# Graph network layer on one core: counting apart from the sort's prefixes, and a strided digit comparison

## What is computed

```python
edge_index = jnp.stack([src, dst])
h = jnp.maximum(_layernorm(x), 0.0)
# attention layer: row = src, col = dst
h = (h @ W).reshape(N, H, C)
alpha = leaky_relu(s_src[row] + s_dst[col])
ex = exp(alpha - m[row])            # m: max(segment maximum by row, 0)
deg = segment_sum(ones(E), row)
denom = segment_sum(ex, row) + (E - deg)[:, None] * exp(-m)
out = segment_sum((ex / denom[row])[:, :, None] * h[col], col) + bias
x = x + out
# second layer: an MLP on (x[row], x[col], edge_attr), summed by row
```

## Time and profile before

| | |
|---|---|
| median of three runs | 5412.68 us |
| profiled execution, its own time | 5404.83 us |
| its span, first to last instruction | 5403.0 us |
| stage 1, start to the first instruction behind its barrier | 297.1 us |
| scatters of stage 2, first start to last start | 316.28 to 2329.63 us |
| mean granted TensorE clock | 0.906 of full |

### The profile page before, as it was taken

How to read it: one execution, slowest core, us unless ns; L and a number is a source line. 1 busy time by engine, 2 the same in 40 slices (tenths; PEclk the granted TensorE clock), 3 DMA queues, 4 the chain that set the end, 5 groups by cost and what they waited for, 6 DMA issues and landing times. The chain is left out here.

```text
span 5403.0 us, 98958 instructions
## 1 busy us (share of the span) xinstructions
PE 4070.9 (75%) x22798; PEld 3396.3 (63%) x22799; DVE 3569.6 (66%) x8071; ACT 3043.6 (56%) x4591; POOL 3250.7 (60%) x3487
## 2 busy tenths in 40 slices
PE   5778777777777777700799987777777777777778
PEld 5766666666666666600799965666666666666666
DVE  8945444444444444429999986777777777777776
ACT  5545555555555555401677756666666666666665
POOL 2357777777777777750000005777777777777774
PEclk9988888888888888855899999999999999999999
DMA  8865555555555554597200046656666666666655
GB/s 311 321 204 151 139 139 140 140 139 141 139 140 142 139 139 139 156 89 19 58 0 0 0 114 162 147 144 147 144 148 144 147 144 147 144 147 144 147 144 134
DMA packets 1212202, 734.52 MB, mean 136 GB/s; under 512 B 929642, under 2 KB 1031204, under 8 KB 1205388
## 3 DMA queue, kind: packets, MB, share of 16 engines
q1 hardware_dynamic: 862700, 336.19, 31.5%
q0 software_dynamic: 131424, 275.52, 17.5%
q10 hardware_dynamic: 218048, 122.49, 7.6%
HBM read 562.32 MB, written 165.09 MB: 135 GB/s over the span
## 5 line engine op out<-in xcount | busy, mean ns | idle before, releaser
L1086 POOL DMA_INDIRECT g_q<-q_d,g_aux x1660 | 1571.3, 947 | 1380.3 <-DMA pw<-g_q 874.7
L577 POOL DMA_INDIRECT rec_d<-rec,place x1568 | 1536.3, 980 | 502.8 <-issue 476.1
L1393 PE MATMUL g_hp<-pw,g_mix 128*128 x3328 | 878.1, 386 | 317.0 <-ACT g_mix L1290 310.8
L690 PE MATMUL lk<-tab_sd,low 128*128 128x196 f32 x3136 | 1050.8, 422 | 0.0
L1404 PE MATMUL g_ap<-g_hid,g_oh 128*128 128x256 f32 x3328 | 876.4, 386 | 133.9 <-DVE agg L1196 129.7
L626 DVE TENSOR_REDUCE rank<-equal 128x4 f32<-128x512 bf16 x392 | 262.4, 684 | 1015.4 <-ACT equal L554 1014.8
L1310 ACT ACTIVATE g_hid<-g_q 128x512 f32<-128x512 f32 x832 | 524.0, 630 | 712.5 <-DVE g_q L1182 699.2
L1393 PEld LDWEIGHTS g_hp<-pw,g_mix 128*128 128x128 f32 x3328 | 617.2, 190 | 475.2 <-issue 399.3
L1182 DVE TENSOR_TENSOR g_q<-g_hp,g_q 128x512 f32<-128x512 f32 x832 | 573.2, 689 | 484.9 <-DMA g_q<-q_d,g_aux 333.9
L687 PE MATMUL lk<-mask,hx 122*128 122x245 bf16 x1568 | 480.0, 306 | 440.2 <-ACT low L543 440.2
L554 ACT ACTIVATE equal<-rk,minus_two 128x512 bf16<-128x512 f32 x392 | 261.5, 685 | 958.9 <-DMA rec_d<-rec,place 643.1
(11 more groups left out here) (251 smaller groups left out, 5035.2 us busy)
## 6 DMA issues: line engine op xcount, KB each, us to landing
low_row<-rows_d SPq DMA_DIRECT2D x392, 256.0 KB
rec_d<-pad ACTq DMA_DIRECT2D x49, 1152.0 KB, 4.3
g_ea<-rec_d SPq DMA_DIRECT2D x208, 256.0 KB, 4.2
rec<-in_ea ACTq DMA_DIRECT2D x196, 256.0 KB
hx_row<-rows_d SPq DMA_DIRECT2D x392, 98.0 KB
g_lrow<-low_row_d SPq DMA_DIRECT2D x208, 128.0 KB, 4.2
g_q<-q_d,g_aux POOLq DMA_INDIRECT x1660, 3.0
rec_d<-rec,place POOLq DMA_INDIRECT x1568
```

The costliest lines, as they stand in the source:

```text
L577: pool.indirect_dma_start(rec_d, bass.IndirectOffsetOnAxis(ap=place[0:n, at, j:j + 1], axis=0), rec[0:n, at, j, :], None).then_inc(s_sc[at ...
L690: mm = pe.matmul(to[:, NB:LK], low[:, par, 1, slots], tab_sd[:, :, :].rearrange("p h a -> p (h a)"), start=False, stop=True, skip_group_ch ...
L1086: pool.indirect_dma_start(qg[:, par, j, :], None, q_d, bass.IndirectOffsetOnAxis(ap=aux[:, par, j, F_IDX - F_LOW:REC - F_LOW].bitcast(I32) ...
L1393: mm = pe.matmul(hp[u][:, k * HID:(k + 1) * HID], mix[:, par, 2 * u + k, :], pw[:, bass.ds(b[k], 1), :].rearrange("p o f -> p (o f)"), sta ...
```

## The change

In stage 1 TensorE now only counts: all 32 matmuls of a step add into one region of 49 PSUM columns (cnt), over all 49 steps, without ever being moved out. The one-hots of 4 groups are made by one pair of VectorE instructions, in two buffers, and the first two steps' pairs stand right behind the source digits, ahead of the statistics. The moves, the stores to pre_d and GpSimd's additions are gone. The prefixes are made in stage 2, one group ahead, from one-hots (ohl, ohh) that VectorE compares with digits held in PSUM; the table addition reads them from PSUM. Groups 0 and 1 are loaded in stage 1, ahead of the h stores. A fill has 26 columns in place of 32, so that SyncE issues 15 of them at the start and ScalarE 49 of the smaller size. The comparison for hx walks its 1024 elements with the 8 columns innermost, a step of 128 elements. Two copies of the record swap places.

```diff
-FILL = 32
+FILL = 26
@@ load_group @@
-                sp.dma_start(pre_in[:, par, :], pre_d[one, :, :].rearrange("o p n -> (o p) n")).then_inc(s_ld[par], 16)
@@ stage 1, sync @@
                     def store(it):
-                        for k in range(FOUR):
-                            g = it * FOUR + k
-                            sp.wait_ge(s_pre, g + 1)
-                            sp.dma_start(pre_d[bass.ds(g, 1), :, :].rearrange("o p n -> (o p) n"), pre[:, k, :]).then_inc(s_ps[k], 16)
                         sp.wait_ge(s_ev, it + 1)
...
+                    sp.wait_ge(s_rowst, 16)
+                    load_group(sp, 0, 0)
+                    load_group(sp, 1, 1)
                     with sp.Fori(0, NB) as it:
                         store(it)
-                    sp.wait_ge(s_rowst, 16)
-                    sp.wait_ge(s_ps[0], 16)
-                    load_group(sp, 0, 0)
-                    for k in range(FOUR):
-                        sp.wait_ge(s_ps[k], 16 * NB)
@@ stage 1, gpsimd @@
-                    def add(it):
-                        for k in range(FOUR):
-                            g = it * FOUR + k
-                            pool.wait_ge(s_pre, g + 1)
-                            pool.sem_inc(s_go, 1)
-                            pool.wait_ge(s_tot, g + 1)
-                            pool.tensor_tensor(tot[:, :], tot[:, :], pre[:, k, (G - 1) * NB:G * NB], ALU.add).then_inc(s_tot, 1)
@@ stage 1, vector @@
+                    def onehots(it, par):
+                        if not first(it, 2):
+                            v.wait_ge(s_hist, it - 1)
+                        of = low_src[:, bass.ds(it * FOUR, FOUR), :]
+                        v.tensor_tensor(oh_low[:, par, :, :, :], of.unsqueeze(2).to_broadcast([P, FOUR, P, G]),
+                                        iota_g[:, :, :].unsqueeze(1).to_broadcast([P, FOUR, P, G]), ALU.is_equal)
+                        of = high_src[:, bass.ds(it * FOUR, FOUR), :].rearrange("p k j -> p (k j)")
+                        v.tensor_tensor(oh_high[:, par, :, :, :].rearrange("p k j a -> p (k j) a"), col(of, P, FOUR * G, NB),
+                                        row(iota_b[:, 0:NB], P, FOUR * G, NB), ALU.is_equal).then_inc(s_oh1, 1)
+
+                    v.wait_ge(s_dig, 2)
+                    onehots(0, 0)
+                    onehots(1, 1)
...
-                    onehot(0, 0)
...
-                    with v.Fori(1, NB) as i:
-                        for k in range(FOUR):
-                            onehot(i * FOUR + k, k)
+                    with v.Fori(1, NB // 2) as i:
+                        onehots(i * 2, 0)
+                        onehots(i * 2 + 1, 1)
+                    onehots(NB - 1, 0)
@@ stage 1, tensor @@
+                    def count(it, par):
+                        pe.wait_ge(s_oh1, it + 1)
+                        for k in range(FOUR):
+                            for j in range(G):
+                                mm = pe.matmul(cnt[:, PRE:PRE + NB], oh_low[:, par, k, :, j], oh_high[:, par, k, j, :],
+                                               start=first(it) and k == 0 and j == 0,
+                                               stop=isinstance(it, int) and it == NB - 1 and k == FOUR - 1 and j == G - 1,
+                                               skip_group_check=True)
                         mm.then_inc(s_hist, 1)
...
                         pe.transpose(tp[:, 0:P], hb[:, :], ident[:, :]).then_inc(s_t, 1)
-                        count(it * FOUR, 0)
-                        count(it * FOUR + 1, 1)
+                        if not last:
+                            count(it + 2, par)
                         pe.wait_ge(s_hT, it + 1)
...
-                        count(it * FOUR + 2, 2)
-                        count(it * FOUR + 3, 3)
+                    count(0, 0)
+                    count(1, 1)
                     pe.wait_ge(s_wx, 1)
@@ stage 1, scalar @@
-                        moved(it, 0)
...
-                        moved(it, 1)
-                        moved(it, 2)
...
-                        moved(it, 3)
                         fill(act, it + EARLY)
...
+                    act.activation(digits, iota[:, :], ACT.Copy)
@@ stage 2, sync @@
-                        sp.wait_ge(s_tab, g - 1)
                         load_group(sp, g, par)
-                    load_group(sp, 1, 1)
@@ stage 2, vector @@
-                    v.tensor_copy(deg[:, :], tot[:, :]).then_inc(s_deg, 1)
+                    v.tensor_copy(deg[:, :], cnt[:, PRE:PRE + NB]).then_inc(s_deg, 1)
+                    def onehots(g, par):
+                        if not first(g, 2):
+                            v.wait_ge(s_cnt, g - 1)
+                        tile = lambda a: a[:, bass.ds(g, 1), :].rearrange("p o j -> p (o j)")
+                        v.tensor_tensor(ohl[:, par, :, :], row(tile(low_src), P, P, G), col(digits, P, P, G), ALU.is_equal)
+                        v.tensor_tensor(ohh[:, par, :, :], col(tile(high_src), P, G, NB), row(digits[:, 0:NB], P, G, NB),
+                                        ALU.is_equal).then_inc(s_oh, 1)
+                    onehots(0, 0)
+                    onehots(1, 1)
...
-                        v.tensor_scalar(hx[0:R_END, par, :], hx_row[0:R_END, par, :], digit[0:R_END, 0:1], None, ALU.is_equal
-                                        ).then_inc(s_hx, 1)
+                        by_slot = lambda a: a[0:R_END, par, :].rearrange("p (j e) -> p e j", j=G)
+                        v.tensor_scalar(by_slot(hx), by_slot(hx_row), digit[0:R_END, 0:1], None, ALU.is_equal).then_inc(s_hx, 1)
...
-                        v.tensor_tensor(tab[:, par, :, :], pre_in[:, par, :].rearrange("p (j a) -> p j a", j=G),
+                        v.wait_ge(s_cnt, g + 1)
+                        v.tensor_tensor(tab[:, par, :, :], cnt[:, 0:PRE].rearrange("p (j a) -> p j a", j=G),
                                         row(tab[:, 1 - par, G - 1, :], P, G, NB), ALU.add).then_inc(s_tab, 1)
...
+                        v.tensor_copy(rec[:, at, :, F_IDX].bitcast(I32), dst_i[:, one, :].rearrange("p o j -> p (o j)"))
                         v.tensor_copy(rec[:, at, :, F_LOW:F_IDX], meta[:, one, :, :].rearrange("p o j f -> p (o j) f"))
-                        v.tensor_copy(rec[:, at, :, F_IDX].bitcast(I32), dst_i[:, one, :].rearrange("p o j -> p (o j)"))
...
                             prepare(i * DEEP + (k + 1), (k + 1) % 2)
+                            onehots(i * DEEP + (k + 2), k % 2)
                             finish(i * DEEP + k, k)
@@ stage 2, tensor @@
+                    def counted(g, par):
+                        pe.wait_ge(s_oh, g + 1)
+                        if not first(g):
+                            pe.wait_ge(s_tab, g)
+                        for j in range(G):
+                            mm = pe.matmul(cnt[:, j * NB:PRE], ohl[:, par, :, j], row(ohh[:, par, j, :], P, G - j, NB),
+                                           start=(j == 0), stop=(j == G - 1), skip_group_check=True)
+                        mm.then_inc(s_cnt, 1)
...
                         matched(g, par, 0)
+                        if not last:
+                            counted(g + 1, 1 - par)
```

More of the change, by code:

```diff
@@ L211, in build @@
                 pick = sb("pick", [P, NB], F32, ctx)
[L212 to L217, removed]
+                oh_low = sb("oh_low", [P, 2, FOUR, P, G], BF16, ctx)
+                oh_high = sb("oh_high", [P, 2, FOUR, G, NB], BF16, ctx)
                 tp, mp = pb("l0_tp", ctx), pb("l0_mp", ctx)
@@ L375, in _, with step @@
                                            op0=ALU.mult, op1=ALU.mult).then_inc(s_rstd, 1)
-                    for k in range(1, FOUR):
-                        onehot(k, k)
-                    with v.Fori(1, NB) as i:
-                        for k in range(FOUR):
-                            onehot(i * FOUR + k, k)
+                    with v.Fori(1, NB // 2) as i:
+                        onehots(i * 2, 0)
+                        onehots(i * 2 + 1, 1)
+                    onehots(NB - 1, 0)
                 @block.tensor
                 def _(pe):
-                    def count(g, k):
-                        pe.wait_ge(s_oh, g + 1)
-                        if not first(g, FOUR):
-                            pe.wait_ge(s_pre, g - (FOUR - 1))
-                        for j in range(G):
-                            mm = pe.matmul(hist[k][:, j * NB:G * NB], oh_low[:, k, :, j],
-                                           row(oh_high[:, k, j, :], P, G - j, NB), start=(j == 0), stop=(j == G - 1),
-                                           skip_group_check=True)
+                    def count(it, par):
[6 more added lines that the diff above has]
+                                               skip_group_check=True)
                         mm.then_inc(s_hist, 1)
-                    def step(it):
+                    def step(it, par, last=False):
                         pe.wait_ge(s_h, it + 1)
```

(16 more changed lines are left out.)

52 lines of the change are left out of this document (20 added, 32 removed).

## The result

The change made the kernel slower: 5647.09 us (median of 4 runs, 5642.36 to 5647.67) against 5414.01 us for the kernel before. The ratio is 1.0433, 95% interval 1.042 to 1.0446. The profiled execution took 5642.36 us, with a span of 5640.5 us and a mean granted clock of 0.896.

The account below looks back on a forecast made before the run. VectorE was taken to bound stage 1 and GpSimd's scatters stage 2. Terms -54 + 3 - 11.4 + 5 = -57 gave 5347 us on the profiled execution (5404.8); forecast 5350 us, range 5327 to 5388.

Parts of the forecast that it names:

- the price of hx with a step of 128: Stage 2: hx excludes GpSimd at two elements a cycle, 0.68 us; 9 us of delays in place of 4.1, +5 us.
- delays' formula: Stage 2: 196 instructions of length d, starts evenly spread, delay scatters by 196 x (d - 0.13)^2 / (2 x 1.271).
- the factor of 0.4: Stage 2: VectorE keeps in step with scatters, so hx costs 0.4 of the evenly spread delays: 9 us at 0.68 us.
- Bound of stage 2: GpSimd's scatters set stage 2, 8 x 1.271 us a group; the other engines have slack.
- Stage 1, VectorE: One-hots of four groups per instruction: steps of 3.90 us in place of 5.17, stage 1's steps ending at 227 us.
- Rival 3: Stage 1: one-hots of four groups lose the pairwise rate, 6 us a step, total 5404 us; chance 0.07.
- Stage 1, DMA and ScalarE: Stage 1: 262 GB/s a step is covered; early fills holding ScalarE cost 2 us, bounds 0 and 20.
- Rival 1: Stage 1: fills holding ScalarE or a lower clock in part, 4.6 to 4.7 us a step, 5381 us; chance 0.15.
- The seam: Between stages: 14 us to the degree, at 243 us (54 earlier); then +3 us to the first scatter, near 265.
- Table addition: Stage 2: reading one operand from PSUM, it no longer delays scatters, -11.4 us (0 at the other bound).
- Stage 2, the rest: Stage 2: other work on VectorE, TensorE and loads lies under 10.17 us a group, effect 0.
- Rival 2: Stage 2: hx excludes scatters at one element a cycle, 1.21 us, 90 us in place of 4.1; 5429 us; chance 0.06.

Follow-up runs that it names:

- e5: Changed kernel with hx walked in pairs, two neighbouring elements and then a step of 128: 5352.87 us (one execution).
- e3: Changed kernel with hx still at a step of 128, but comparing two tensors, the digit read from PSUM: 5415.71 us (one execution).
- e7: e1 with fills of 32 columns as before, in place of 26: 5332.21 us, ratio 0.9864 to the kernel before.
- e1: Changed kernel with hx walked in order again, without the step, nothing else different: 5328.05 us, ratio 0.9861 to the kernel before.
- e4: Changed kernel with hx contiguous and the digit read from PSUM: 5324.24 us, ratio 0.9853 to the kernel before.
- e6: e1 with stage 2's low one-hots compared with digits in SBUF, both inputs in SBUF: 5364.92 us, ratio 0.9923 to the kernel before.
- e9: e4 plus an unread load of 98 KB a group in stage 2: 5322.59 us, ratio 0.9848 to the kernel before.
- e2: Kernel before the change with only hx's step of 128 put in: 5738.21 us (one execution), 335 above the kernel before.

## Why the prediction was wrong

The step that failed is **the price of hx with a step of 128**. It was taken at 0.68 us, bounded above by one element a cycle, 1.21 us; it measured 2.53 us. Its term in the sum was +5 us; held scatters made it some 304 (307.6 us of delays by hx, 3.9 before). The upper bound was no bound: it took for granted that the engine reads and writes at full rate whatever the distance, and a row for that (two neighbours of a 16-bit pair fetched from places 256 bytes apart) was not in the trace. L637, which I named for a large step, moves whole 4-byte words. It could not show it, and e5 shows that whole words cost little. That hx goes on excluding was right, as the held scatters show; that it takes two elements at a time fits the ratio of 4.72 to 2.53 us, but isn't proven. The Trainium skill's rule ("Vector Engine (DVE) Microarchitecture Reference", 5.1), that the mode with both ports asks no step of 1, agrees with the trace: with a step of 128 elements hx still held 194 scatters.

With that length the **delays' formula** leaves its field. The share of groups in which a start falls into hx, d/1.271, can't exceed 1, and at 2.53 us 194 of the 196 hx hold a scatter; the other two run ahead of the first one. The line itself changes too. The delay is what is left of VectorE's instruction less 0.13 us for the contiguous ones and for e5's, but less 0.63 us in the changed kernel, the median of 144 scatters that start inside hx. And 50 more start up to half a microsecond ahead of it and are held as well. Timeline of the changed kernel, GpSimd, then VectorE:

```profile
1201.69 2.90 POOL L548 DMA_INDIRECT rec_d<-rec,place  x1 [0.30 <-issue]
...
1201.98 2.50 DVE L593 TENSOR_SCALAR hx<-hx_row,digit 122x1024 bf16<-122x1024 bf16 x1
```

This scatter starts 0.29 us ahead of hx and loses 1.94 us. From its start to hx's end are 2.79 us, so it loses that less 0.85; the median of the 50 is 0.84. This second line holds for short ones too, and matters little there: in the trace of before, with hx at 0.49 us, starts 0.3 us ahead lost nothing and starts 0.45 us ahead lost 0.08.

The 0.63 is not a matter of length alone. Timeline of the kernel before, VectorE, then GpSimd, at the one long addition outside the groups:

```profile
2296.81 6.68 DVE L666 TENSOR_TENSOR xb<-xb,bias_b 128x6272 f32<-128x6272 f32 x1
...
2297.95 6.39 POOL L577 DMA_INDIRECT rec_d<-rec,place  x1 [0.30 <-issue]
```

What is left of it is 5.54 us, and the scatter loses 5.42, less by 0.12. Nor is it a matter of the kind of instruction alone, since the contiguous hx keeps to 0.13. Whether the large step makes it, or the length for this kind, no run tells apart. By the two lines of the changed kernel evenly spread starts lose 1.65 us on average (0.49 us of the period of 1.265 at 1.92 us, the other 0.775 at 1.49), 324 us for 196; measured were 307.6. My line would have given 1.76 us each, 346, so with the right length the forecast would have had the sign and nearly the size.

A smaller step failed as well: **the factor of 0.4**, by which VectorE's keeping in step was to spare hx most of the even spread. At e5's length, 0.69 us, the formula gives 24 us for evenly spread starts, and hx cost 23. So even at 0.68 us the term would have been near +19 and not +5.

Point by point:

- **Bound of stage 2** (GpSimd's scatters, with slack elsewhere): right. It is also why an exclusion, not a wait, cost the time: idle "issue" is about 476 us in every row of the scatters shown but e3's.
- **Stage 1, VectorE**: 3.90 us a step predicted, 3.90 measured. Rival 3, the lost pairwise rate, did not come: 4096 elements took 2.28 us.
- **Stage 1, DMA and ScalarE**: no engine was held by fills, at 414 GB/s or with 32 tiles a fill (e7). Rival 1 did not come, nor a lower clock.
- **The seam**: degree at 243 predicted, 240.53 measured; first scatter at 265, measured 261.49 (258.86 in e1). That the first hx is slower accounts for part of the last difference.
- **Table addition**: -11.4 us predicted. The one example above starts inside it and is not held; in e4, where hx too reads PSUM, two scatters over 1.0 us remain in all, the first one and the one at xb. Right. The Trainium skill's inference ("SBUF — State Buffer", Who interferes with whom), that a two-input instruction does not stall descriptor generation, fails here once more: e6's one-hot has both inputs in SBUF and added 37 us of delays.
- **Stage 2, the rest**: 0 predicted. True for the slack, but the quiet step shortened by 9 ns (in e1; by 6 in the changed kernel), a gain of 13 us that no term held. Together with the -57.4 and the delays this makes e1 75 us faster (77 by the spans), where my sum without hx was 54 - 3 + 11.4 = 62.
- **Rival 2** named the right mechanism, exclusion that outweighs the gains, and put its turning point at 1.0 us. At its worst price of 1.21 it ended at 5429; the real price was twice that, so even the rival was 218 us short. The 0.06 for slower followed from the same bound. The range's upper end, 5388, did not hold even that: it was put together from rival 1 and the table's term at 0 (which add up to 5392), with hx left at 0.68 us, while the prediction's own upper price of hx led to 5429. (By its formula the turning point, 62 us more than before, lies at 1.06 us, not 1.0.)
- **The tail**: 8.5 us more behind the last scatter in the changed kernel, 3 in e1. It lies in parts that the change doesn't touch, and I did not follow it.

## What to carry to other kernels

Before a 16-bit instruction is given a pattern whose innermost step is large, price the jumps (here they made 2.53 us of 0.51), or keep two neighbours together innermost (0.69). Where GpSimd's descriptors set the time, price each VectorE instruction by whether it excludes GpSimd, not by its length: one operand in PSUM made it 0.7 us longer and spared every scatter. And a price that no row shows has no upper bound taken from the rate of other patterns; a tight bound there should cost the forecast some of its confidence.

## What the runs showed of the hardware that was not expected

- 1024 bf16 elements compared with one value on VectorE: 0.51 us contiguous, 0.69 us in pairs that jump every 4 bytes, 2.53 us with a jump of 256 bytes between any two; against an operand in PSUM 1.22 and 4.72 us.
- A scatter that starts inside an excluding contiguous instruction loses what is left of it less 0.13 us, of 0.5 us as of 6.68 us; inside the 2.53 us hx with its large step it is less 0.63 us. One that starts up to half a microsecond ahead is held too, and loses the time to the instruction's end less 0.84 us. So a scatter seems to need the shared resource at its start and again about half a microsecond on; that reading is inferred from the delays.
- The instruction right behind the hx with a step takes longer: `ohl`, unchanged, took 1.41 us there and 1.43 in e3, against 1.21 in e1 and e4.
- Two excluding instructions back to back hold a scatter for both (1.71 us in e6).
- On TensorE a moving operand of 49 bf16 columns with a step of 8 elements made 32 products take 3.20 us instead of 2.16, at a granted clock of 1.00 in both.
- The quiet step of the scatters went from 1.271 to 1.2625 us with the change for a reason that is not the removed load (e9). It is 1.2713 us in e2, so most of it goes with the rest of the change and not with hx. But it is 1.265 in the changed kernel, e5 and e6, and 1.2625 in e1, which differs from them in one line, so it doesn't go with the rest of the change alone.
